# Corner keys of late attention units gathered by GpSimd into one tile, in a vision-transformer layer kernel

## The chip, the cores and the metric

The kernel runs on one core of a Trainium2 chip. The time is the device time of one execution in microseconds (us); several executions are timed and the median counts. TensorE multiplies matrices and transposes (a product with the identity), ScalarE (ACT) and VectorE (DVE) read its results from PSUM, GpSimd (POOL) works on SBUF, SyncE (SP) issues DMAs. The engines run their own instruction streams in order and wait for one another through semaphores.

## The reference

One layer of a vision transformer over 64 images of 197 tokens (196 patches and a class token) with 192 features:

```
h = concat(cls_tok, patches(x) @ W_proj.T + b_proj)
z = layernorm(h)
for e in range(4):                       # 4 experts, 12 heads of 16 features each
    q, k, v = z @ wq[e].T, z @ wk[e].T, z @ wv[e].T
    s = q @ k.T / 4, kept where 0 <= i - j < 64     # sliding window over keys
    outs.append((softmax(s) @ v) @ wo[e].T)
f = concat(outs)
h = h + silu(f @ w_gate.T) * (f @ w_up.T)
z = layernorm(h)
expert = argmax(softmax(z @ gate_w + gate_b - gate_center))
h = h + (gelu(z @ w1[expert] + b1[expert]) @ w2[expert] + b2[expert])
```

## The kernel before

After a prologue (weights are split into a high and a low half-precision part) a loop `Fori` of 32 turns takes two images a turn; an expert stage follows it. A turn projects q, k and v, writes them to SBUF, and SyncE's DMAs (`stack_queries`, `stack_keys`) gather them in the layout that the score products need. Then the attention runs as a pipeline of `UNITS` = 64 units (`unit_of`): 8 groups of 6 heads, and in each group 8 units: first the four of the first 128 queries, then the four "late" ones of the last 69 queries; each has three heads (`HU`) of one image. In what follows a group's units are numbered 0 to 7, the late ones 4 to 7.

In step s of the pipeline each engine does, in this order of its own:

- TensorE: `scores(s)` (the mask and the scores, L706 and L711, into one of three banks), `patch_part` (embedding of the next turn, in early steps only, L263), `turn_p(s - 2)` (transposes of the probabilities, L728 and L731, into one of three banks), `times_v(s - 5)` (products of the turned probabilities with v, at L245 by `product`)
- ScalarE: the copy of the turned probabilities in half precision (`pt_hi`, L838) for unit s - 3, then the exponentials of unit s (`p_ready`, L847)
- VectorE: every fourth step the copy of the output bank to `o_raw` (`o_copied`, L921), then the minimum of the scores of unit s (L928), the low part of unit s - 4 by subtraction (`pt_lo`, L933), and every fourth step the reciprocals (L942)
- GpSimd: for each window of four units `divide(w)`: the sum of two halves of `o_raw` (L874, when `o_copied`), then the multiply with the reciprocals (L880, when `o_rcp_ready`)

The output of four units lies in one PSUM bank, so that the first product of the next window waits for `o_copied`. `scores(s)` waits for the exponentials of unit s - 3, `turn_p(u)` for those of unit u and for `pt_lo` of unit u - 3.

A late query needs keys 65 to 196 (`KWN[1]` = 132). 128 keys fit on the partitions: 69 to 196. The four others (`EDGE`), keys 65 to 68, matter to the first four of the late queries alone. Before, each head of a late unit is therefore transposed twice: once for its first 128 keys, of which four columns are kept (L728), and once for its last 128 (L731); `times_v` then multiplies both with their v, in a high and a low part, four products a head. The v of the edge keys stands in `v[:, img, 1]`, where a DMA at L661 puts it on partitions 0 to 3 and the rest is zero.

Of the kernel before, what the change touches and what calls it, by code (L numbers as in the profile page):

```python
# [52 lines left out]
PTN = (128, TOK - 128 + EDGE)  # L53
PT2 = 2 * (TOK - 128)
# [29 lines left out]
def unit_of(u):  # L84

    return u // 8, u // 4 % 2, u // 2 % 2, u % 2
# [7 lines left out]
def vit_layer(nc, x_t, wp, tok_bias, wqkv, wo, wgu, gate_w, gate_bc, w1, b1, w2, b2, ident, mask_id,  # L94
# [4 lines left out]
    with ExitStack() as ctx:  # L99
# [8 lines left out]
        def sem(name):  # L108
# [61 lines left out]
        pt_late = w1_s[:].rearrange("p s b e n -> p (s b e n)")[:, 0:PR * 2 * HU * PT2].rearrange(  # L170
            "p (r s n) -> p r s n", r=PR, s=2)
        gated = pt_f[:, 0:8 * D].bitcast(F32).rearrange("p (t d) -> p t d", t=4)
# [30 lines left out]
            proj_mm proj_hi proj_lo v_dup stacked0 stacked1 stacked2 scores_mm min_ready p_ready pt_mm pt_hi pt_lo pv_mm  # L203
# [276 lines left out]
        with nc.Block() as block:  # L480
# [20 lines left out]
            def _(dve):  # L501
# [17 lines left out]
                nc.vector.memset(pt_late, 0.0)  # L519

# [59 lines left out]
        def probs(u, hl):  # L580

            if unit_of(u)[1]:
                return pt_late[:, u % PR, hl].rearrange("p (h n) -> p h n", h=HU)
            return pt[:, u % PR, hl, 0:HU * 128].rearrange("p (h n) -> p h n", h=HU)

        def turned_probs(u):
            half = unit_of(u)[1]
            n = PT2 if half else 128
            return bank[T_BANK + u % TR][:, 0:HU * n].rearrange("p (h n) -> p h n", h=HU)[:, :, 0:PTN[half]]

# [4 lines left out]
        LAG_T, LAG_HI, LAG_LO, LAG_PV = 2, 3, 4, 5  # L595
# [32 lines left out]
        with nc.Fori(0, STEPS, hint_back_edge=True) as i:  # L628
            with nc.Block(no_gpsimd_drain=True) as block:

                @block.sync
                def _(sp):
# [25 lines left out]
                    for img in range(PAIR):  # L658

                        sp.wait_ge(S["proj_lo"], v_first + 2 * img + 2)  # L660
                        sp.dma_start(v[0:EDGE, img, 1], v[KW0[1]:KW0[1] + EDGE, img, 0]).then_inc(S["v_dup"], 16)  # L661
# [7 lines left out]
                def _(pe):  # L669
# [46 lines left out]
                    def turn_p(u):  # L716
# [6 lines left out]
                        else:  # L723
                            pe.wait_ge(S["proj_lo"], last_use(T_BANK + u))
                        for j in range(HU):
                            c0, k0 = j * (PT2 if half else 128), j * kn
                            if half:
                                nc.tensor.transpose(turned[:, c0 + rows:c0 + 2 * rows], p_slot(u)[:, k0:k0 + 128],  # L728
                                                    ident_s[0:rows, 0:rows])
                                k0 += EDGE  # L730
                            mm = nc.tensor.transpose(turned[:, c0:c0 + rows], p_slot(u)[:, k0:k0 + 128],  # L731
# [586 lines left out]
```

## Time and profile before

| | us |
|---|---|
| median of 3 runs | 4598.94 (4598.64 to 4599.28) |
| the profiled execution | 4602.34 |
| its span, from the first to the last instruction | 4600.4 |
| TensorE busy | 4002.9 (87%) |
| VectorE busy | 3501.7 (76%) |
| ScalarE busy | 3061.3 (67%) |
| GpSimd busy | 1094.2 (24%) |
| mean granted TensorE clock | 0.968 |

A row of a timeline gives the start in us, the duration, the engine, the line, the operation with what it writes and reads, how many instructions are merged, and in brackets how long the engine sat idle before it and who released it. Durations of products contain the latency of the engine's pipeline; what a product costs the next one is the distance of their starts. PE is TensorE's products, PEld its weight loads.

### The profile page before, as it was taken

How to read it: one execution, taken by the hardware profiler on the slowest of the kernel's cores; microseconds unless marked ns; L12 is line 12 of the kernel's file. 1: busy time of each engine (PE TensorE's matmuls, PEld its weight loads, DVE VectorE, ACT ScalarE, POOL GpSimd, SP SyncE). 2: the span in 40 equal slices, each digit the busy share in tenths (PEclk: the TensorE clock that was granted, in tenths of full speed). 3: DMA queues.
4: the chain of work that ended last, by engine and by line, in shares of the span. 5: the costliest groups of instructions: out<-in, count | busy, mean ns of one | idle time of the engine just before them, and what ended most of it. 6: DMA issues, size and time to landing. Idle time of an engine off the chain costs nothing. (4 is left out here: it accounts for less than half of the span.)

```text
span 4600.4 us, 129415 instructions
## 1 busy us (share of the span) xinstructions
PE 4002.9 (87%) x47470; PEld 3077.7 (67%) x47470; DVE 3501.7 (76%) x8872; ACT 3061.3 (67%) x9620; POOL 1094.2 (24%) x1496
## 2 busy tenths in 40 slices
PE   3889888888888898888888889888888888896998
PEld 2677666666666776666666667666666666774776
DVE  4788777777777887777777778777777777785665
ACT  2777766666777777666666777776666667772433
POOL 0222222222222222222222222222222222221222
PEclk7999999999999999999999999999999999997999
DMA  5122221111111222211111112222111111124664
GB/s 180 38 50 50 50 50 48 45 45 47 45 30 45 50 50 50 50 46 45 46 47 44 31 46 50 50 50 50 45 47 46 46 33 40 48 50 167 223 217 162
DMA packets 241812, 294.02 MB, mean 64 GB/s; under 512 B 56489, under 2 KB 223955, under 8 KB 231554
## 3 DMA queue, kind: packets, MB, share of 16 engines
q1 hardware_dynamic: 217698, 214.47, 18.2%
q10 hardware_dynamic: 4608, 38.73, 2.5%
q0 software_dynamic: 18912, 32.58, 2.0%
q8 instruction: 412, 6.75, 0.6%
q14 instruction: 182, 1.49, 0.1%
HBM read 127.06 MB, written 43.10 MB: 37 GB/s over the span
## 5 line engine op out<-in xcount | busy, mean ns | idle before, releaser
L847 ACT ACTIVATE p_s<-bank,smin 128x128 f32<-128x128 f32 (+1 forms) x6144 | 1825.3, 376 | 228.8 <-DVE smin L928 218.3
L928 DVE TENSOR_REDUCE smin<-bank 128x3 f32<-128x384 f32 (+1 forms) x2048 | 1140.7, 557 | 306.1 <-PE bank L711 271.8
L731 PE MATMUL bank<-ident_s,p_s 128*128 128x128 f32 (+1 forms) x6144 | 1008.6, 252 | 17.7
L731 PEld LDWEIGHTS bank<-ident_s,p_s 128*128 128x128 f32 (+1 forms) x6144 | 727.2, 142 | 89.3 <-issue 60.7
L706 PE MATMUL bank<-masks_s,mask_id_s 128*128 128x384 f16 (+1 forms) x2048 | 676.3, 330 | 30.7 <-DVE qt_f L899 16.3
L711 PE MATMUL bank<-stacks_f 128*128 128x256 f16 (+3 forms) x4096 | 678.8, 247 | 0.0
L728 PE MATMUL bank<-ident_s,p_s 69*128 69x69 f32 x3072 | 508.6, 233 | 140.2 <-DVE pt_f L933 133.4
L874 POOL TENSOR_TENSOR w_s<-o_raw 128x192 f32<-128x192 f32 (+1 forms) x512 | 307.4, 600 | 1242.9 <-DVE o_raw L921 1242.9
L728 PEld LDWEIGHTS bank<-ident_s,p_s 69*128 69x128 f32 x3072 | 399.8, 141 | 260.3 <-issue 235.4
L245 PEld LDWEIGHTS bank<-v_f,w_s 128*69 128x69 f16 x12288 | 549.7, 116 | 25.1 <-issue 3.8
L245 PE MATMUL bank<-v_f,w_s 128*69 128x33 f16 x12288 | 560.8, 186 | 5.8
L933 DVE TENSOR_TENSOR pt_f<-bank,pt_f 128x384 f16<-128x384 f32 x1024 | 557.0, 544 | 0.0
L245 PE MATMUL bank<-zt,wqkv_s 128*128 128x394 f16 x1920 | 404.4, 374 | 174.1 <-PEq L983 164.3
L711 PEld LDWEIGHTS bank<-stacks_f 128*128 128x128 f16 (+1 forms) x4096 | 431.0, 105 | 123.3
L838 ACT CAST pt_f<-bank 128x384 f16<-128x384 f32 x1024 | 505.8, 494 | 0.0
L245 PEld LDWEIGHTS bank<-zt,wqkv_s 128*128 128x128 f16 x1920 | 203.7, 109 | 356.4 <-issue 259.7
L880 POOL TENSOR_TENSOR w_s<-w_s,o_rcp 128x192 f32<-128x192 f32 (+1 forms) x512 | 261.5, 511 | 714.5 <-DVE o_rcp L942 712.0
L933 DVE TENSOR_TENSOR w_s<-bank,w_s 128x219 f16<-128x219 f32 x1024 | 383.5, 377 | 30.0 <-ACT w_s L838 30.0
L838 ACT CAST w_s<-bank 128x219 f16<-128x219 f32 x1024 | 369.3, 361 | 54.6 <-PE bank L731 52.7
L772 PE MATMUL bank<-wgu_s,qt_f 128*128 128x384 f16 (+1 forms) x2304 | 400.6, 326 | 0.0
L921 DVE COPY o_raw<-bank 128x396 f32<-128x396 f32 (+1 forms) x512 | 289.1, 565 | 79.0 <-PE bank L245 53.4
L245 PE MATMUL bank<-v_f,pt_f 128*128 128x33 f16 x6144 | 314.8, 178 | 0.0
(124 smaller groups left out, 5471.2 us busy)
## 6 DMA issues: line engine op xcount, KB each, us to landing
stacks_f<-qt_f SPq DMA_DIRECT2D x768, 73.9 KB, 2.1
stacks_f<-kt_f SPq DMA_DIRECT2D x1536, 36.9 KB, 2.1
wx_t<-wx_d SPq DMA_DIRECT2D x36, 1344.0 KB
x_raw<-x_t_dram ACTq DMA_DIRECT2D x32, 1182.0 KB
rec_t<-rec_d SPq DMA_DIRECT2D x36, 678.0 KB, 4.1
rec_d<-fill_s SPq DMA_DIRECT2D x5, 678.0 KB, 4.1
stacks_f<-w_dram SPq DMA_DIRECT2D x2, 1536.0 KB
wx_d<-w_s SPq DMA_DIRECT2D x8, 384.0 KB
```

Of the source, the lines that this page charges most:

```text
L245: mm = nc.tensor.matmul(psum, stat, mov, start=(n == 0), stop=(n == len(passes) - 1))
L706: nc.tensor.matmul(ps, mask_id_s[:, 0:rows], masks_s[:, m0:m0 + HU * kn], start=True, stop=False)
L711: mm = nc.tensor.matmul(ps[:, j0 * kn:j1 * kn], qst[:, g % QS, two, q0:q0 + rows], kst[:, g % KS, h0 + j0:h0 + j1, k0:k0 + kn], start=Fals ...
L728: nc.tensor.transpose(turned[:, c0 + rows:c0 + 2 * rows], p_slot(u)[:, k0:k0 + 128], ident_s[0:rows, 0:rows])
L731: mm = nc.tensor.transpose(turned[:, c0:c0 + rows], p_slot(u)[:, k0:k0 + 128], ident_s[0:rows, 0:rows])
L772: mm = nc.tensor.matmul(bank[GU_BANKS[tt]][0:rows, 0:2 * D], ot[:, b, zi, c0:c0 + rows], wgu_s[:, s, b, :], start=(b == 0 and s == zi == 0 ...
L838: nc.scalar.copy(probs(u, 0)[:, :, 0:PTN[half]], turned_probs(u)).then_inc(S["pt_hi"], 1)
L847: ins = nc.scalar.activation(p_slot(s)[:, j * kn:j * kn + kn], bank[s % SR][0:rows, j * kn:j * kn + kn], ACT.Exp, scale=-1.0, bias=smin[0: ...
L874: nc.gpsimd.tensor_tensor(mine, o_raw[0:rows, w % 2, :, :, 0:HD], o_raw[0:rows, w % 2, :, :, HD:2 * HD], ALU.add).then_inc(S["o_summed"], 1)
L921: nc.vector.tensor_copy(o_raw[0:rows, w % 2], o_bank(rows)).then_inc(S["o_copied"], 1)
L928: nc.vector.tensor_reduce(least, ps, AX_X, ALU.min).then_inc(S["min_ready"], 1)
L933: nc.vector.tensor_tensor(probs(u, 1)[:, :, 0:PTN[half]], turned_probs(u), probs(u, 0)[:, :, 0:PTN[half]], ALU.subtract).then_inc(S["pt_lo ...
```

## The change

GpSimd copies, for each late unit, the 4 x 4 corners of its three heads (four queries by four edge keys) side by side into `edges`, a tile of which the rest is zero. It does so in step s for unit s - 1, ahead of a division that falls in the same step. TensorE waits for that copy (`edge_ready`), transposes the tile once, which puts head j's edge keys on partitions 4j to 4j + 3, and then each head's last 128 keys. The v of the edge keys is laid out to match: six DMAs in place of two put head j's rows on partitions 4j to 4j + 3. In `times_v` one product with 99 columns (three heads by 33) adds the edge part of all three heads, once for the high and once for the low part. A late unit has four transposes in place of six and eight products in place of twelve; the copy of its turned probabilities has 211 columns in place of 219.

```diff
-PTN = (128, TOK - 128 + EDGE)
-PT2 = 2 * (TOK - 128)
+EDGE_STEP = EDGE
+PTN = (HU * 128, HU * (TOK - 128) + EDGE)
+PT2 = (HU + 1) * (TOK - 128)
...
+        edges = w1_s[:].rearrange("p s b e n -> p (s b e n)")[:, PR * 2 * PT2:PR * 2 * PT2 + XR * 256].bitcast(
+            F32).rearrange("p (r n) -> p r n", r=XR)
...
                 nc.vector.memset(pt_late, 0.0)
+                nc.vector.memset(edges, 0.0)
...
-                        sp.dma_start(v[0:EDGE, img, 1], v[KW0[1]:KW0[1] + EDGE, img, 0]).then_inc(S["v_dup"], 16)
+                        for j in range(HU):
+                            sp.dma_start(v[EDGE_STEP * j:EDGE_STEP * j + EDGE, img, 1, j::HU],
+                                         v[KW0[1]:KW0[1] + EDGE, img, 0, j::HU]).then_inc(S["v_dup"], 16)
...
+                        if half:
+                            pe.wait_ge(S["edge_ready"], edge_of(u) + 1)
+                            nc.tensor.transpose(turned[:, HU * rows:HU * rows + rows], edges[0:rows, u % XR],
+                                                ident_s[0:rows, 0:rows])
                         for j in range(HU):
-                            c0, k0 = j * (PT2 if half else 128), j * kn
-                            if half:
-                                nc.tensor.transpose(turned[:, c0 + rows:c0 + 2 * rows], p_slot(u)[:, k0:k0 + 128],
-                                                    ident_s[0:rows, 0:rows])
-                                k0 += EDGE
-                            mm = nc.tensor.transpose(turned[:, c0:c0 + rows], p_slot(u)[:, k0:k0 + 128],
-                                                     ident_s[0:rows, 0:rows])
+                            k0 = j * kn + kn - 128
+                            mm = nc.tensor.transpose(turned[:, j * rows:j * rows + rows],
+                                                     p_slot(u)[:, k0:k0 + 128], ident_s[0:rows, 0:rows])
...
                         if u == 4:
-                            pe.wait_ge(S["v_dup"], 32)
+                            pe.wait_ge(S["v_dup"], 16 * PAIR * HU)
...
+                        h0 = HG * g + HU * hh
+                        o = o_bank(rows)[:, img, HU * hh:HU * hh + HU, :]
+                        if half:
+                            nc.tensor.matmul(o, probs(u, 0)[:, HU * rows:PT2], v[:, img, 1, h0:h0 + HU, :],
+                                             start=True, stop=False)
                         for j in range(HU):
-                            head = HG * g + HU * hh + j
-                            o = o_bank(rows)[:, img, HU * hh + j, :]
-                            passes = [(probs(u, hl)[:, j, rows * b:rows * b + rows], v[:, img, 2 * half - b, head, :])
-                                      for b in range(1 + half) for hl in range(2)]
-                            mm = product(o, passes)
+                            for hl in range(2):
+                                mm = nc.tensor.matmul(o[:, j], probs(u, hl)[:, j * rows:j * rows + rows],
+                                                      v[:, img, 2 * half, h0 + j, :],
+                                                      start=(hl == 0 and not half), stop=(hl == 1 and not half))
+                        if half:
+                            mm = nc.tensor.matmul(o, probs(u, 1)[:, HU * rows:PT2], v[:, img, 1, h0:h0 + HU, :],
+                                                  start=False, stop=True)
                         mm.then_inc(S["pv_mm"], 1)
...
-                    for w in range(2 * G):
-                        divide(w)
+                    for s in range(PIPE):
+                        u = s - LAG_EDGE
+                        if 0 <= u < UNITS and unit_of(u)[1]:
+                            pool.wait_ge(S["p_ready"], u + 1)
+                            if u >= XR:
+                                pool.wait_ge(S["pt_mm"], u - XR + 1)
+                            nc.gpsimd.tensor_copy(edges[0:EDGE, u % XR, 0:HU * EDGE],
+                                                  split_heads(p_slot(u)[0:EDGE])[:, :, 0:EDGE]
+                                                  ).then_inc(S["edge_ready"], 1)
+                        w = window_at(s, LAG_OC)
+                        if w is not None:
+                            divide(w)
```

`LAG_EDGE` is 1, and `LAG_OC` stays 6. `edge_of(u)` counts the late units. The ScalarE copy and the VectorE subtraction take the same tiles as before, now without a dimension for the head.

## Rows read from the trace of the kernel before

**Rows 1.** Busy time by stretch: one period of eight units.

```profile
core 0: us, PE busy (x) PEld busy (x) DVE busy (x) ACT busy (x) POOL busy (x), PEclk, DMA share, GB/s
2040.23:2049.81 9.58, 8.88 (x139) 7.25 (x135) 8.48 (x21) 9.08 (x33) 2.22 (x4) 1.00 0.22 46
```

**Rows 2.** Timeline of turn 16, scores of unit 1 to scores of unit 4.

```profile
2040.23 0.32 PE L706 MATMUL bank<-masks_s,mask_id_s 128*128 128x384 f16 x1
...
2041.55 0.32 PE L706 MATMUL bank<-masks_s,mask_id_s 128*128 128x384 f16 x1
...
2042.55 0.38 DVE L933 TENSOR_TENSOR w_s<-bank,w_s 128x219 f16<-128x219 f32 x1
2042.66 0.32 PE L706 MATMUL bank<-masks_s,mask_id_s 128*128 128x384 f16 x1
...
2042.84 0.22 DVE L942 RECIPROCAL o_rcp<-o_raw 128x12 f32<-128x12 f32 x1
2043.07 0.52 PE L731 MATMUL bank<-ident_s,p_s 128*128 128x128 f32 x3
2043.19 0.56 DVE L928 TENSOR_REDUCE smin<-bank 128x3 f32<-128x384 f32 x1
...
2043.42 0.56 PE L245 MATMUL bank<-v_f,w_s 128*69 128x33 f16 x12
...
2043.83 0.34 PE L706 MATMUL bank<-masks_s,mask_id_s 128*69 128x396 f16 x1
```

**Rows 3.** Timeline of the same turn, exponentials of unit 5 onward.

```profile
2046.40 0.89 ACT L847 ACTIVATE p_s<-bank,smin 69x132 f32<-69x132 f32 x3 [0.17 <-DVE smin L928]
2046.75 0.56 DVE L928 TENSOR_REDUCE smin<-bank 69x3 f32<-69x396 f32 x1
2046.98 0.25 PE L728 MATMUL bank<-ident_s,p_s 69*128 69x69 f32 x1 [0.28 <-DVE pt_f L933]
...
2047.23 0.55 DVE L933 TENSOR_TENSOR pt_f<-bank,pt_f 128x384 f16<-128x384 f32 x1
...
2047.69 0.21 DVE L942 RECIPROCAL o_rcp<-o_raw 69x12 f32<-69x12 f32 x1
...
2047.92 0.25 PE L728 MATMUL bank<-ident_s,p_s 69*128 69x69 f32 x1
...
2048.05 0.51 POOL L880 TENSOR_TENSOR w_s<-w_s,o_rcp 69x192 f32<-69x192 f32 x1 [1.49 <-DVE o_rcp L942]
...
2048.32 0.31 PE L245 MATMUL bank<-v_f,pt_f 128*128 128x33 f16 x6
2048.48 0.32 PE L706 MATMUL bank<-masks_s,mask_id_s 128*128 128x384 f16 x1
...
2048.64 0.33 PE L711 MATMUL bank<-stacks_f 128*128 128x256 f16 x2
...
2049.81 0.32 PE L706 MATMUL bank<-masks_s,mask_id_s 128*128 128x384 f16 x1
...
2050.00 0.57 DVE L921 COPY o_raw<-bank 128x396 f32<-128x396 f32 x1
...
2050.72 0.56 PE L245 MATMUL bank<-v_f,w_s 128*69 128x33 f16 x12
```

**Rows 4.** GpSimd's timeline in the projection part of the same turn.

```profile
2005.05 4.69 POOL L886 TENSOR_TENSOR x_s<-x_raw,x_s 128x2364 f16<-128x2364 f32 x1 [6.11 <-ACT x_s L826]
2009.67 0.51 POOL L887 COPY h_in<-h_next 128x384 f32<-128x384 f32 x1
2010.12 0.51 POOL L888 COPY h_in<-h_next 69x384 f32<-69x384 f32 x1
```

**Rows 5.** SyncE's timeline (the time to issue), around the duplicates of v.

```profile
2008.38 1.33 SPq L661 DMA_DIRECT2D v_f<-v_f  x2
...
2015.58 3.88 SPq L652 DMA_DIRECT2D stacks_f<-kt_f  x6
2026.71 1.88 SPq L640 DMA_DIRECT2D stacks_f<-qt_f  x3
```

**Rows 6.** Busy time by stretch (columns as in rows 1): projection part of a turn.

```profile
2004.80:2006.60 1.80, 0.02 (x1) 0.00 (x0) 1.15 (x3) 1.80 (x6) 1.55 (x1) 1.00 0.42 85
2008.60:2012.00 3.40, 3.40 (x13) 1.71 (x12) 3.03 (x10) 1.08 (x3) 2.03 (x3) 0.56 0.23 46
```

More of the change, by code:

```diff
@@ L169, in vit_layer @@
         pt = pt_f[:].rearrange("p (r s n) -> p r s n", r=PR, s=2)
-        pt_late = w1_s[:].rearrange("p s b e n -> p (s b e n)")[:, 0:PR * 2 * HU * PT2].rearrange(
+        pt_late = w1_s[:].rearrange("p s b e n -> p (s b e n)")[:, 0:PR * 2 * PT2].rearrange(
             "p (r s n) -> p r s n", r=PR, s=2)
+        edges = w1_s[:].rearrange("p s b e n -> p (s b e n)")[:, PR * 2 * PT2:PR * 2 * PT2 + XR * 256].bitcast(
+            F32).rearrange("p (r n) -> p r n", r=XR)
         gated = pt_f[:, 0:8 * D].bitcast(F32).rearrange("p (t d) -> p t d", t=4)
@@ L202, in vit_layer @@
         names = """patch_mm embedded z1_ready z2_ready z1t_mm z1t_hi z1t_lo z2t_mm z2t_hi z2t_lo var_ready rstd_ready
-            proj_mm proj_hi proj_lo v_dup stacked0 stacked1 stacked2 scores_mm min_ready p_ready pt_mm pt_hi pt_lo pv_mm
+            proj_mm proj_hi proj_lo v_dup stacked0 stacked1 stacked2 scores_mm min_ready p_ready edge_ready pt_mm pt_hi pt_lo pv_mm
             o_copied o_summed o_rcp_ready o_ready ot_mm ot_hi ot_lo gu_mm sig_ready dve_own h_moved
@@ L580, in probs, with edge_of @@
         def probs(u, hl):
-            if unit_of(u)[1]:
-                return pt_late[:, u % PR, hl].rearrange("p (h n) -> p h n", h=HU)
-            return pt[:, u % PR, hl, 0:HU * 128].rearrange("p (h n) -> p h n", h=HU)
+            return pt_late[:, u % PR, hl] if unit_of(u)[1] else pt[:, u % PR, hl, 0:PTN[0]]
         def turned_probs(u):
-            half = unit_of(u)[1]
-            n = PT2 if half else 128
-            return bank[T_BANK + u % TR][:, 0:HU * n].rearrange("p (h n) -> p h n", h=HU)[:, :, 0:PTN[half]]
+            return bank[T_BANK + u % TR][:, 0:PTN[unit_of(u)[1]]]
+        def edge_of(u):
+            return u // 8 * 4 + u % 4
         def split_heads(ap):
             return ap.rearrange("p (h k) -> p h k", h=HU)
-        LAG_T, LAG_HI, LAG_LO, LAG_PV = 2, 3, 4, 5
+        LAG_EDGE, LAG_T, LAG_HI, LAG_LO, LAG_PV = 1, 2, 3, 4, 5
         LAG_OC, LAG_OR = 6, 7
@@ L837, in _ @@
                                 act.wait_ge(S["pv_mm"], u - PR + 1)
-                            nc.scalar.copy(probs(u, 0)[:, :, 0:PTN[half]], turned_probs(u)
+                            nc.scalar.copy(probs(u, 0)[:, 0:PTN[half]], turned_probs(u)
                                            ).then_inc(S["pt_hi"], 1)
@@ L932, in _ @@
                             dve.wait_ge(S["pt_hi"], u + 1)
-                            nc.vector.tensor_tensor(probs(u, 1)[:, :, 0:PTN[half]], turned_probs(u),
-                                                    probs(u, 0)[:, :, 0:PTN[half]], ALU.subtract
+                            nc.vector.tensor_tensor(probs(u, 1)[:, 0:PTN[half]], turned_probs(u),
+                                                    probs(u, 0)[:, 0:PTN[half]], ALU.subtract
                                                     ).then_inc(S["pt_lo"], 1)
```

## The prediction

> **What bounds the kernel now.** The loop over 32 pairs of images takes most of the span, and its attention part is a pipeline of 64 units in which TensorE, VectorE and ScalarE hand each unit round in a fixed order. I read first the busy time of one period of eight units [rows 1]: 9.58 us, of which TensorE is busy 8.88, ScalarE 9.08, VectorE 8.48 and GpSimd 2.22. No engine is full, so a sum of removed busy time would tell little: the period has to be walked. The timeline of that period [rows 2, 3] shows how. Numbering the units of a group of heads 0 to 7 (4 to 7 are the late ones, 69 queries), the rows from 2041.55 to 2043.83 are steps in which TensorE goes from product to scores to transposes without a break: there its work is the limit. The rows at 2046.98 and 2049.81 to 2050.72 are others: TensorE waits for VectorE's subtraction (0.28 us idle before unit 4's transposes), and unit 4's product waits for the copy that empties the output bank. Time saved on TensorE counts in the first kind of step, not in the second. Last I looked at where GpSimd stands in time, because the change makes TensorE wait for it.
>
> **TensorE's saving.** A late unit now has six transposes, whose starts lie 0.0625 us apart (2047.92 to 2048.32 is 0.40 for six) [rows 3]; four remain: -0.125 us. It has twelve value products, 0.41 us from the first to the next scores (2043.42 to 2043.83) [rows 2], 0.0345 each; eight remain, two of them 99 columns wide. No row has 99 columns behind 69-column weights. The mask's product streams 384 columns in 0.16 (2048.48 to 2048.64) [rows 3], so 99 take 0.041. The lower bound is the narrow product's own 0.0345 (the wide one costs nothing more), the upper 0.0345 + 0.041 = 0.075 (one after the other). I take 0.049, near the streaming time, for weights load beside the stream before: 6 x 0.0345 + 2 x 0.049 = 0.305, so -0.11 us. The Trainium skill, "TensorE: Matmul & The Clock Gate", section "LDWEIGHTS (loading the stationary operand)", says that a weight load costs by its columns alone; by it 69-column weights are never dearer than 128-column ones, so that all small products would cost 0.026 and a late unit's saving would be 12 x 0.026 - (6 x 0.026 + 2 x 0.043) = 0.07 and not 0.11; with 20 such savings a turn on the path the sum would come out 25 us higher. The trace disagrees: six products with 128-column weights take 0.16 us, 0.026 each [rows 3], and those with 69 columns take 0.0345.
> Together 0.235 us for each of 32 late units a turn. Walking the period without any new wait, one transposition saving (0.125; the others fall into steps that wait for VectorE) and two product savings (0.22) reach the path: 0.345 a group. In the first 15 steps of a turn, where the patch products ride along, TensorE is the limit throughout and 0.81 us is saved. That gives 0.81 + 6 x 0.345 = 2.9 us a turn, 93 us in all, if GpSimd were free.
>
> **The new wait.** It is not free. GpSimd's queue is now, in step order: copy of unit 4's corners, both halves of the division of the late units before, copy of unit 5, 6, 7, division of units 0 to 3. The copy for unit 5 thus stands behind the division's multiply, which waits for the reciprocal. In the trace unit 5's transposes start at 2047.92 and the multiply only at 2048.05; it ends at 2048.56 [rows 3]. The copy's own input has been ready since 2047.29 (0.89 us of exponentials from 2046.40). Behind TensorE's new wait are queued: unit 5's transposes, the product of unit 2, and the scores of the next group's unit 0, on which VectorE and ScalarE depend.
> The delay: 0.13 (multiply starts after the transposes) + 0.45 (GpSimd's multiply to its next instruction; two of its copies start 0.45 apart though each lasts 0.51 [rows 4]) + the copy + the hand-over. No row of GpSimd is as small as 12 columns on 4 partitions. Its rows of two inputs, 192 columns in 0.51 and 2364 in 4.69 [rows 3, 4], make 1.92 ns a column and 0.14 fixed; the upper bound is the 384-column copy, 0.51; the lower, below that fixed part, 0.10. I take 0.19, near the fixed part since 12 columns add 0.02. The hand-over to TensorE: VectorE's copy of the bank ends at 2050.57 and TensorE starts at 2050.72, 0.15 [rows 3]; for GpSimd I take 0.175, bounds 0.11 and 0.20 (no row has TensorE waiting for GpSimd). So 0.13 + 0.45 + 0.19 + 0.175 = 0.95 us, the first time. [...]
> It happens where a late division precedes: in seven of the eight groups of heads of a turn.
>
> **What a period then takes.** From unit 5's transposes to the next group's, with the longest link each time:
> - four transposes 0.25, product of unit 2 0.15, then scores of unit 0 to VectorE's minimum 0.53 (as 2042.66 to 2043.19) [rows 2], minimum 0.48, late subtraction 0.29 (as 2042.55 to 2042.84), copy of the output bank 0.57 and hand-over 0.15 (2050.00 to 2050.72) [rows 3]: 2.42
> - product of unit 4, 0.305; then two steps of scores, minimum, subtraction, transposes, product: 0.53 + 0.48 + 0.38 + 0.15 + 0.35 (2043.07 to 2043.42) + 0.305 = 2.19: together 2.50
> - scores of unit 4 to minimum 0.55 (0.02 more than above, 12 columns more), minimum 0.48, wide subtraction 0.46, bank copy 0.57, hand-over 0.15, product 0.15: 2.36
> - scores of unit 6 to minimum 0.55, minimum 0.48, subtraction 0.46, reciprocal to multiply 0.36 (2047.69 to 2048.05), multiply 0.45, copy 0.19, hand-over 0.175: 2.67
> Sum 9.95; with the unrounded starts 9.90. Before: 9.58 (2040.23 to 2049.81) [rows 2, 3]. The chain now runs once through every engine, and costs +0.32 a group in spite of the savings in it.
> A turn: -0.81 (opening) + 0.95 (first hold) + 6 x 0.32 (periods between seven holds) - 0.82 (behind the last one: three transposition and four product savings) = +1.24 us; times 32 turns, +40 us.
>
> **The rest.** The other three copies are hidden: unit 5's exponentials end at 2047.29, 0.63 us ahead of its transposes [rows 3], and I take the others for alike; start of GpSimd 0.15 after its releaser (reciprocal's end 2047.90 to 2048.05), copy 0.19 and hand-over 0.175 make 0.51. Should it not fit, each costs its excess only. The copy of unit 4 delays the addition before the multiply by 0.2 us, covered by 1.49 us in which the multiply waits for the reciprocal [rows 3]. ScalarE's copy and VectorE's subtraction lose 8 of 219 columns, under 0.01 us each, beside other work. SyncE issues six duplicating DMAs in place of two, +4 x 0.67 = 2.7 us on its queue [rows 5]; the last key stack behind them ends at 2022.2 and not 2019.46, and that queue next waits until 2026.71, so they are covered; without that cover it would be 2.7 us a turn. The two buffers' memsets come once and add under 1 us.
>
> **Sum.** 4602.3 us (profiled execution) + 40 = 4642; that execution is 3.4 us over the median, so 4639.
>
> **Rivals.**
> A, forecast: the held period, 4639. Its own range: copy 0.10 gives 0.09 less for each of 224 holds, -20 us; copy 0.51 gives +72; wide product 0.0345 or 0.075 gives -0.03 or +0.05 at 20 places a turn, -19 or +33. 4605 to 4700. Chance 0.62.
> B, faster: the hold doesn't form, and all of TensorE's saving stays: 4599 - 93 = 4506. It decides at GpSimd's multiply: were it done before about 2047.5, the copy would be ready when TensorE asks. For it: the multiply waits 1.49 us for a reciprocal that VectorE could give sooner if TensorE's lead moved it; and the hold lets VectorE catch up. Against: 2048.56 in the trace, and VectorE's order puts the reciprocal behind two instructions of the same step. In between (a part of the hold repaid) any time from 4506 to 4590. Chance 0.20.
> C, no change: hold as in A with every open term at its low end (copy 0.10, hand-over 0.11, narrow price for wide products): 224 x 0.155 + 19 = 54 us less than A, 4585; with one of them nearer its middle 4590 to 4608. Chance 0.10.
> D, much slower: TensorE idles some 1.1 us in every period, and the clock falls. After a stretch in which TensorE had almost nothing for 1.8 us the granted clock fell to 0.56, in the projection part of a turn; in the attention part it is 1.00, with idle times of 0.3 [rows 1, 3, 6]. At half clock for one third of each period TensorE-bound steps would add about 0.8 us a group, 200 us for 256 groups: 4840, and with one group in four 4690. The Trainium skill, "TensorE: Matmul & The Clock Gate", section "HAM oscillation — how this bites in real kernels", tells of kernels that lose the clock by waits in every round. Chance 0.08.
>
> **From these the numbers.** Predicted 4639. Range 4585 to 4695: it takes A nearly whole and C, and leaves out most of B and D. A measurement of this kernel can tell 0.2% (9 us) from no change. Faster 0.20 (B), same 0.10 (C), slower 0.70 (A and D).
>
> **What would show it.** In the trace after: TensorE idle about 1.1 us before unit 5's edge transpose, released by GpSimd's copy, in seven groups a turn, and a period of 9.9 us; GpSimd's copy near 0.19 us, its start 0.45 behind the multiply's; eight late products in 0.305. Wrong if the copy takes over 0.3 us, if the clock falls in the attention part, or if the multiply moves ahead so that the hold is under 0.5 us.

## The result: 2.4% slower

The changed kernel takes 4708.94 us, the median of four runs (4702.35 to 4718.34), beside 4598.99 for the kernel before on the same chip: ratio 1.0241, 95% interval 1.0223 to 1.0258. It is slower, as forecast, but by 110 us and not by 40, and outside the range of 4585 to 4695. The profiled execution took 4702.35 us (span 4700.5); its mean granted clock is 0.941, where it was 0.968.

From the page of the changed kernel: busy times, the granted clock by slices, and the groups of the new transpose and of GpSimd's new copy (shapes and count | busy us, mean ns of one | idle us before, and what ended it).

```profile
PE 3907.5 (83%) x41326; PEld 2901.9 (62%) x41326; DVE 3491.1 (74%) x8873; ACT 3051.2 (65%) x9620; POOL 1247.3 (27%) x2520
PEclk7999999999999999999989999999999999997999
L734 PE MATMUL bank<-ident_s,w_s 69*128 69x69 f32 x1024 | 260.1, 254 | 317.9 <-POOL w_s L910 220.1
L910 POOL COPY w_s<-p_s 4x12 f32<-4x12 f32 x1024 | 176.6, 183 | 807.2 <-ACT p_s L861 804.8
```

TensorE is busy for 95 us less than before, at a time that is 100 us longer. What took its place stands in the list of its waits (us in total, times, longest):

```profile
PE bank L734 <- POOL w_s L910: 220.1, 221, 1.2
```

Of 224 holds that were forecast (seven a turn), 221 are seen, 1.0 us each: the first of a turn has 1.2 us of idle time, the six behind it 0.96. One of these, in the timeline of turn 11, is the answer to [rows 3]; the second fence is the same place one period on:

```profile
1451.80 0.21 DVE L966 RECIPROCAL o_rcp<-o_raw 69x12 f32<-69x12 f32 x1
...
1452.15 0.51 POOL L894 TENSOR_TENSOR w_s<-w_s,o_rcp 69x192 f32<-69x192 f32 x1 [1.30 <-DVE o_rcp L966]
...
1452.61 0.31 POOL L910 COPY w_s<-p_s 4x12 f32<-4x12 f32 x2
...
1452.93 0.25 PE L734 MATMUL bank<-ident_s,w_s 69*128 69x69 f32 x1 [0.96 <-POOL w_s L910]
...
1453.37 0.32 PE L713 MATMUL bank<-masks_s,mask_id_s 128*128 128x384 f16 x1
```
```profile
1462.82 0.25 PE L734 MATMUL bank<-ident_s,w_s 69*128 69x69 f32 x1 [0.96 <-POOL w_s L910]
```

GpSimd starts the multiply 0.14 us after the reciprocal's end, the copy of unit 5's corners 0.46 behind the multiply's start, and TensorE starts 0.32 after that (the copy's 0.18 and a hand-over of 0.145). From hold to hold 9.89 us pass.

To see where the 100 us went I split each turn in two: the attention part, from the scores of unit 0 to the last product of unit 63, and the projection part, up to the next turn's scores. The windows below (stretch, length, busy time of each engine with its count, granted clock, DMA share, GB/s) are four attention parts, the first of the kernel before and three of the kernel after; then two projection parts of the kernel after.

```profile
2018.04:2102.04 84.00, 78.39 (x1150) 66.11 (x1151) 70.98 (x171) 73.88 (x260) 21.10 (x34) 1.00 0.22 57
```
```profile
3370.92:3455.66 84.74, 72.62 (x959) 58.36 (x959) 70.62 (x171) 73.40 (x260) 25.91 (x66) 1.00 0.24 60
1412.87:1498.46 85.59, 73.80 (x959) 59.62 (x960) 70.68 (x171) 73.39 (x260) 25.92 (x66) 0.98 0.23 58
2320.62:2409.80 89.18, 77.62 (x958) 62.85 (x959) 70.62 (x171) 73.97 (x260) 25.92 (x66) 0.92 0.23 57
...
1498.46:1542.52 44.06, 34.98 (x226) 20.62 (x224) 28.80 (x85) 16.12 (x32) 9.51 (x9) 0.88 0.10 19
1629.44:1671.83 42.39, 32.90 (x227) 19.90 (x224) 28.66 (x85) 16.13 (x32) 9.52 (x9) 0.96 0.08 16
```

With the full clock (2.4 GHz) all through, an attention part takes 84.74 us, 0.75 more than before. But in 30 of the 32 turns the clock falls to its lower level (1.2 GHz) in some stretches, and the part takes up to 5.3 us more. Summed over the 32 turns:

- the attention parts went from 2688.9 to 2773.1 us, +84. Of that 32 x 0.75 = 24 is the longer walk, the forecast's own mechanism. The other 61 go with the clock: in all, 205 us of the attention parts lie at the lower level, where the kernel before has none.
- the 31 projection parts between turns went from 1323 to 1340 us, +17. They come in two lengths, 44.1 and 42.4 us, and the long one occurs 16 times and not 4 (one of the expectations below has 17 and 5).
- the rest of the span differs by 1 us.

In what follows two of the four sets of runs (e1_mult_later to e4_longer_turn, and e6 to e9_longer_again) were taken in a condition in which the kernel before, too, takes 4693 to 4696 us. The kernel before has no trace in it; in every trace of the other kernels there, each turn has a stall of about 1.3 us between its units 5 and 6, and often a stretch of slow clock right behind it. Ratios are therefore taken within a set, and the slow clock is counted from 20 us into the attention part onward. One of the four executions of e8_filled_again took 16966 us, the others 4769 to 4775, and its ratio is that of the others.

### The profile page after: what moved, and what is told of

Its sections match the earlier page's. It is cut to its first block and busy times, and to the rows that moved or that the text cites. A ratio compares the mean times of both kernels' runs of the same rounds, so it can differ in the third digit from the quotient of the medians.

```text
span 4700.5 us, 119304 instructions
## 1 busy us (share of the span) xinstructions
PE 3907.5 (83%) x41326; PEld 2901.9 (62%) x41326; DVE 3491.1 (74%) x8873; ACT 3051.2 (65%) x9620; POOL 1247.3 (27%) x2520
## 5 line engine op out<-in xcount | busy, mean ns | idle before, releaser
L738 PE MATMUL bank<-ident_s,p_s 128*128 128x128 f32 (+1 forms) x6144 | 908.7, 259 | 31.0 <-DVE pt_f L957 11.8
L713 PE MATMUL bank<-masks_s,mask_id_s 128*128 128x384 f16 (+1 forms) x2048 | 692.8, 338 | 30.8 <-DVE qt_f L923 16.4
L738 PEld LDWEIGHTS bank<-ident_s,p_s 128*128 128x128 f32 (+1 forms) x6144 | 627.2, 147 | 134.1 <-issue 103.6
L718 PE MATMUL bank<-stacks_f 128*128 128x256 f16 (+3 forms) x4096 | 700.4, 253 | 0.0
L734 PE MATMUL bank<-ident_s,w_s 69*128 69x69 f32 x1024 | 260.1, 254 | 317.9 <-POOL w_s L910 220.1
L734 PEld LDWEIGHTS bank<-ident_s,w_s 69*128 69x128 f32 x1024 | 150.2, 147 | 455.3 <-ACT p_s L861 228.4
L852 ACT CAST w_s<-bank 128x211 f16<-128x211 f32 x1024 | 362.2, 354 | 67.4 <-PE bank L738 63.2
L957 DVE TENSOR_TENSOR w_s<-bank,w_s 128x211 f16<-128x211 f32 x1024 | 376.2, 370 | 39.1 <-ACT w_s L852 39.1
L910 POOL COPY w_s<-p_s 4x12 f32<-4x12 f32 x1024 | 176.6, 183 | 807.2 <-ACT p_s L861 804.8
L760 PE MATMUL bank<-v_f,w_s 128*69 128x33 f16 x6144 | 368.7, 188 | 0.0
```

The source lines that it names most:

```text
L713: nc.tensor.matmul(ps, mask_id_s[:, 0:rows], masks_s[:, m0:m0 + HU * kn], start=True, stop=False)
L718: mm = nc.tensor.matmul(ps[:, j0 * kn:j1 * kn], qst[:, g % QS, two, q0:q0 + rows], kst[:, g % KS, h0 + j0:h0 + j1, k0:k0 + kn], start=Fals ...
L734: nc.tensor.transpose(turned[:, HU * rows:HU * rows + rows], edges[0:rows, u % XR], ident_s[0:rows, 0:rows])
L738: mm = nc.tensor.transpose(turned[:, j * rows:j * rows + rows], p_slot(u)[:, k0:k0 + 128], ident_s[0:rows, 0:rows])
L760: mm = nc.tensor.matmul(o[:, j], probs(u, hl)[:, j * rows:j * rows + rows], v[:, img, 2 * half, h0 + j, :], start=(hl == 0 and not half), ...
L852: nc.scalar.copy(probs(u, 0)[:, 0:PTN[half]], turned_probs(u)).then_inc(S["pt_hi"], 1)
```

## The experiments

| kernel | median us | ratio to before in its set | slow clock past 20 us, us in all | undisturbed attention part, us | long projection parts of 31 |
|---|---|---|---|---|---|
| before, b_again, b_third | 4599 to 4602 | | 0, 0, 0 | 83.98 | 4, 3, 4 |
| after | 4708.94 | 1.0241 | 205 | 84.74 | 16 |
| a_again | 4725.74 | 1.0277 [1.0260, 1.0294] | 198 | 84.77 | 27 |
| a_third | 4721.52 (one run) | | 229 | 84.76 | 22 |
| e1_mult_later | 4557.80 | 0.9712 [0.9696, 0.9728] | 0 | 80.8, stall in it | 11 |
| e1_again | 4479.85 | 0.9739 [0.9722, 0.9755] | 0 | 79.62 | 17 |
| e2_filled_hold | 4739.37 | 1.0104 [1.0087, 1.0121] | 0 | 86.2, stall in it | 15 |
| e8_filled_again | 4772.50 | 1.0163 [1.0142, 1.0183] | 0 | 86.3, stall in it | 25 |
| e3_twelve_products | 4624.64 | 0.9862 [0.9839, 0.9884] | 3 | 82.6, stall in it | 15 |
| e4_longer_turn | 4720.18 | 1.0064 [1.0046, 1.0083] | 7 | 84.8, stall in it | 14 |
| e9_longer_again | 4737.09 | 1.0086 [1.0069, 1.0104] | 14 | 85.1, stall in it | 19 |
| e9_third | 4667.32 (one run) | | 0 | 83.97 | 22 |
| e5_hold_alone | 4704.09 | 1.0225 [1.0208, 1.0242] | 0 | 87.30 | 2 |
| e6_long_hold_alone | 4837.63 | 1.0292 [1.0272, 1.0312] | 61 | 89.5, stall in it | 12 |
| e7_hold_twelve | 4910.15 | 1.0465 [1.0439, 1.0491] | 287 | 88.7, stall in it | 17 |
| e7_third | 4790.58 (one run) | | 283 | none; 87.49 with one slow stretch | 13 |

The theory behind the forecast was that the hold costs what the walk of the period says. After the result a second part was needed, that the idle time of the hold lowers the clock. Its rivals were that the lighter load of TensorE lowers it (fewer products), that a longer turn alone does, and, for the projection parts, that the four additional DMAs do.

**Taking the hold away.** The multiply moves one step later in GpSimd's order, behind the corner copy of unit 5; the addition stays. Everything else is the changed kernel.

```diff
-                    def divide(w):
+                    def add(w):
...
+                    def divide(w):
...
                         pool.wait_ge(S["o_summed"], w + 1)
...
                         w = window_at(s, LAG_OC)
                         if w is not None:
+                            add(w)
+                        w = window_at(s, LAG_OR)
+                        if w is not None:
                             divide(w)
```

> The changed kernel with GpSimd's multiply of a division one pipeline step later, so that the corner copy of a group's second late unit runs ahead of it; nothing else differs. Theory (the hold of TensorE behind the multiply costs 0.7 us a turn by itself and pulls the clock down as well): no hold, granted clock 1.00 in the whole attention part, period of eight units about 9.2 us and not 9.9, and the forecast's 2.9 us a turn come out: about 4505 us. Rival 1 (fewer products and transposes thin TensorE's work everywhere and the clock falls for that reason): the clock still falls in the attention part, time 4550 to 4600. Rival 2 (the wait for any GpSimd copy is the trouble, not its place behind the multiply): time stays above 4650.

> The changed kernel with the multiply one step later, once more, beside the changed kernel on one chip. Theory: 2.5 to 3% faster than the kernel before and 4 to 5% faster than the changed one; undisturbed attention part 81.0 us (or 1.3 less on a chip without the early stall, that is 79.7 to 81.1). Rival (its gain of the last call was that chip's): ratio to the kernel before within 0.99 to 1.01.

Measured: 4479.85 us beside 4599.96, and 0.948 of the changed kernel of the same set. The list of waits of e1_again has no wait of TensorE for GpSimd any more, and all 32 attention parts take 79.6 us at the full clock. Waits of e1_again, then one attention part of it:

```profile
POOL w_s L916 <- ACT p_s L861: 955.6, 800, 2.8
PE bank L734 <- DVE pt_f L966: 75.6, 224, 0.6
```
```profile
1345.98:1425.59 79.61, 73.31 (x958) 58.49 (x959) 70.53 (x171) 72.57 (x260) 26.38 (x66) 1.00 0.26 64
```

GpSimd now waits for ScalarE's exponentials, as it should, and unit 4's transposes again wait for VectorE. Fewer products alone do not lower the clock. Ratio and clock came as expected, and both rivals are out. The time of 4505 us that the first of the two texts had did not: it was 4558 in the disturbed set, and 4480 in the undisturbed one, 25 us better than that. The timeline of e1_again has the corner copy and the eight late products:

```profile
1385.28 0.18 POOL L916 COPY w_s<-p_s 4x12 f32<-4x12 f32 x1 [0.82 <-ACT p_s L861]
...
1386.16 0.20 PE L756 MATMUL bank<-v_f,w_s 128*69 128x99 f16 x1
...
1386.20 0.35 PE L760 MATMUL bank<-v_f,w_s 128*69 128x33 f16 x6
...
1386.40 0.21 PE L764 MATMUL bank<-v_f,w_s 128*69 128x99 f16 x1
...
1386.45 0.33 PE L713 MATMUL bank<-masks_s,mask_id_s 128*128 128x384 f16 x1
```

The eight go by in 0.29 us. With six narrow ones at 0.0345 that leaves 0.04 for each wide one, the time its 99 columns stream.

**Filling the hold.** The changed kernel, with six products of 384 columns ahead of the wait in every hold; their result is overwritten. TensorE is kept at work while it would wait, and the hold itself stays.

```diff
+                        if u % 8 == 5 and u > 8:
+                            for _ in range(6):
+                                nc.tensor.matmul(turned[:, 0:384], mask_id_s[:, 0:128], masks_s[:, 0:384],
+                                                 start=True, stop=True)
                         if half:
                             pe.wait_ge(S["edge_ready"], edge_of(u) + 1)
```

> The changed kernel with its hold left as it is, but TensorE runs six products of the mask (384 columns each, 0.16 us, results overwritten) in the hold of each group, ahead of the wait for GpSimd's copy. Theory (the clock falls because TensorE idles 1.2 us in the hold): attention part at granted clock 1.00, its length 84.7 to 85 us a turn, total 4620 to 4640 us. Rival (the clock falls for another reason, or the slower clock is not what costs): clock still below 1.00 in the attention part and 4690 to 4720 us.

> The changed kernel with six products of the mask in each hold, once more on the chip of this call. Theory (idle time in the hold, with the rest, brings the clock down): no slow stretch between 30 and 90 us of a turn, attention part 85.0 us, time 4635 to 4655, 60 to 90 us less than the changed kernel although TensorE does more. Rival: 4700 or more.

The additional work is 6 x 0.16 us, about as long as the idle time. The expected times (4620 to 4640, 4635 to 4655) were missed: 4739 and 4772 us, in sets in which the kernel before takes 4693 and 4696, and the changed kernel did not run in them. The kernel with the filled hold is nearer to the one before than the changed kernel is, 1.010 and 1.016 against 1.024 and 1.028 of other sets, so what the filling saves in time is not shown. The delay is still there: 86.2 us, less the stall of about 1.3, is 84.9, beside 84.74 for the changed kernel. What is firm is the clock: past the first 20 us no slow stretch is left in either of the two traces, against 198 to 229 us in the three of the changed kernel. An attention part of e8_filled_again, its last 62.91 us and then its first 25, which hold the stall, has a clock under 1.00 in the first 25 alone:

```profile
1196.54:1259.45 62.91, 58.46 (x736) 44.55 (x737) 52.98 (x128) 55.41 (x197) 17.98 (x50) 1.00 0.15 32
1171.54:1196.54 25.00, 22.14 (x264) 19.12 (x264) 17.71 (x45) 18.47 (x64) 8.03 (x16) 0.93 0.45 124
```

So the delay of the hold costs the walk, and its idleness costs the clock; the two come apart.

**The products alone.** The kernel of e1 with the narrow products of before, twelve a late unit, on the gathered corners.

```diff
-                        if half:
-                            nc.tensor.matmul(o, probs(u, 0)[:, HU * rows:PT2], v[:, img, 1, h0:h0 + HU, :],
-                                             start=True, stop=False)
...
+                            if half:
+                                for hl in range(2):
+                                    mm = nc.tensor.matmul(o[:, j], probs(u, hl)[:, HU * rows:PT2],
+                                                          v[:, img, 1, h0 + j, :], start=False, stop=(hl == 1))
```

> As the kernel with the later multiply, but with the twelve narrow value products of before in place of eight, so that of TensorE's two savings only the transposes remain. Theory (walk of the period: one transposition saving of 0.125 us a group on the path, none of the products): about 1.1 us a turn less than before, 4563 us, some 58 us more than with eight products. Rival (the transposes are hidden behind VectorE throughout, the products bring it all): 4595 to 4600.

It takes 67 us more than e1_mult_later: 1.8 us in an undisturbed attention part, 60 us over all 32 with their slow stretches, and the rest outside of them. Of what e1 gains over the kernel before in an attention part, 4.37 us (4.0 beside e4_longer_turn, whose attention is that of before, in the same disturbed set), 1.8 thus come from the wide products and 2.2 to 2.6 from the transposes. The expectation had the products about right (58 us) and the transposes at 1.1 us, less than half of that.

**A longer turn alone.** The kernel before, with a VectorE memset of the 1024 columns of `z`, unused at that point, at the end of a turn.

```diff
                         nc.vector.tensor_tensor(h[0:rows, tt, :], h_in[0:rows, tt, :], gu, ALU.add)
+                    nc.vector.memset(z[:], 0.0)
```

> The kernel before with one more memset (1024 columns, about 0.5 to 1.1 us) on VectorE at the end of each turn; attention as before. It asks where 17 us of the projection part come from: in the changed kernel that part of a turn takes 44.1 and not 42.4 us in 17 of 31 turns, before in 5 of 31. Theory (whether the slower clock falls on the projections depends on the length of a turn alone): +16 to +34 us for the memset itself, and the number of long projection parts changes too, up to another 20 us. Rival (those long parts come from the new DMAs or copies): 5 or 6 long parts as before, and the memset's own time alone.

> The kernel before with the memset at the end of a turn, once more: in the call before last it could not be told from that chip's early stall what belonged to it. The kernel before has 3 to 5 of 31 projection parts that are 1.7 us longer, the changed one 16 to 27, and the one with the later multiply 17, though none of them touches the projections. Theory (the length of a turn decides how many are slow): attention part 84.0 us in all turns, more than 8 long projection parts, ratio 1.010 to 1.016. Rival (the new DMAs or copies bring them): 3 to 5 long parts, ratio 1.006 to 1.009.

The first two of these were hard to read because of the stall, seen here in e4_longer_turn at a place where VectorE waits for no semaphore:

```profile
517.50 0.57 DVE L928 TENSOR_REDUCE smin<-bank 69x3 f32<-69x396 f32 x1 [1.64 <-issue]
```

> The kernel before with the memset at the end of a turn, beside the kernel before on one chip. Theory (the length of a turn decides how many projection parts are slow): at least twice as many of the 1.7 us longer ones as the kernel before has on the same chip. Rival: as many as the kernel before, plus or minus two.

By its ratio, 1.0086, e9_longer_again lies with the rival (1.006 to 1.009), by its 19 long parts with the theory, and the two cannot be told apart there. The third, in an undisturbed set with b_third, is clearer, though each is a single run. An attention part and two projection parts of e9_third, then a projection part of b_third:

```profile
1404.95:1488.94 83.99, 78.37 (x1150) 66.09 (x1151) 71.00 (x171) 73.89 (x260) 21.11 (x34) 1.00 0.22 57
...
1488.94:1534.16 45.22, 35.13 (x225) 20.90 (x224) 29.96 (x86) 16.13 (x32) 9.54 (x9) 0.89 0.12 24
1618.15:1661.70 43.55, 33.59 (x225) 20.45 (x224) 29.59 (x86) 16.12 (x32) 9.54 (x9) 0.92 0.11 22
```
```profile
1467.40:1509.86 42.46, 33.62 (x226) 20.44 (x225) 28.67 (x85) 16.11 (x32) 9.53 (x9) 0.92 0.11 22
```

The attention part is untouched, and its clock too: a longer turn doesn't lower it. But the projection part, besides its 1.1 us for the memset, is long in 22 of 31 turns against 4. The kernel takes 65 us more than b_third, of which the memset is 32 x 1.1 = 35 and the long projection parts are 18 x 1.7 = 31. This kernel has no additional DMA, so these aren't needed for the long projection parts.

**A hold alone.** The kernel before, in which TensorE, ahead of unit 5's transposes, waits for the multiply of the division (e5), or for a 12-column GpSimd copy of an otherwise unused tile right behind that multiply (e6). No transposition and no product is saved.

```diff
                             pe.wait_ge(S["proj_lo"], last_use(T_BANK + u))
+                        if u % 8 == 5 and u > 8:
+                            pe.wait_ge(S["o_ready"], u // 8 * 2)
```

In e6 the wait is for `S["edge_ready"]`, which the copy increments.

```diff
                         divide(w)
+                        if w % 2 == 1 and w < 15:
+                            nc.gpsimd.tensor_copy(pad[:, 1], pad[:, 0]).then_inc(S["edge_ready"], 1)
```

> The kernel before with the hold and nothing else: TensorE waits, ahead of the six transposes of a group's second late unit, until GpSimd's multiply of the last division is done; no corner copy, no saving. It measures the wait by itself. Theory (walk of the period with a wait of 0.66 us behind the multiply's start): 3.1 us a turn, 99 us, and the clock falls in the attention part as in the changed kernel, 40 to 80 us more: a ratio of 1.03 to 1.04 to the kernel before. Rival (the hold is mostly repaid in the period, and the clock falls for TensorE's lighter load): ratio 1.00 to 1.02 and clock 1.00 between 30 and 90 us of a turn.

> The kernel before with a hold as long as the changed kernel's: behind the multiply GpSimd copies 12 columns of a tile of its own on 4 partitions, and TensorE waits for that ahead of the six transposes of a group's second late unit. All of TensorE's old work stays. In the hold alone without that copy TensorE idled 0.66 us and the attention part kept its clock; in the changed kernel it idles 0.96 us and the clock falls. Theory A (the length of the hold decides): clock below 1.00 between 30 and 90 us of a turn, 1.035 to 1.05 of the kernel before. Theory B (the hold and TensorE's lighter load are needed together): clock 1.00 there, attention part 88.0 to 88.4 us, ratio 1.028 to 1.033.

Timeline and one attention part of e5_hold_alone:

```profile
1456.97 0.51 POOL L882 TENSOR_TENSOR w_s<-w_s,o_rcp 69x192 f32<-69x192 f32 x1 [1.49 <-DVE o_rcp L944]
...
1457.63 0.25 PE L730 MATMUL bank<-ident_s,p_s 69*128 69x69 f32 x1 [0.66 <-POOL w_s L882]
```
```profile
1416.45:1503.76 87.31, 78.38 (x1150) 66.00 (x1151) 70.95 (x171) 74.45 (x260) 21.07 (x34) 1.00 0.21 54
```

With an idle time of 0.66 us (0.92 once a turn, at the first hold) the clock stays up in all 32 turns, and the kernel pays for the delay alone: 3.33 us an attention part, 104 us in all; the walk had said 3.1 and 99. The 40 to 80 us that the expectation added for the clock did not come. Two attention parts of e6, where the idle time is 0.80 us (1.06 at the first hold):

```profile
1457.14:1546.67 89.53, 78.60 (x1150) 66.00 (x1151) 70.88 (x171) 74.93 (x260) 22.02 (x41) 1.00 0.21 54
1993.13:2087.68 94.55, 83.91 (x1150) 71.00 (x1151) 71.26 (x171) 75.30 (x260) 22.02 (x41) 0.93 0.20 52
```

The clock falls past the first 20 us in 8 of the 32 turns, 61 us in all. Neither theory holds as written: the ratio of 1.0292 is that of B and under A's 1.035, while the clock does fall, which B ruled out, but far less than in the changed kernel. The load of TensorE is the one of before, and so the idle time can suffice without the lighter load. The evidence is thinner than for the filled hold: e6 is of a disturbed set, in which kernels without a hold have 0 to 14 us of such clock (e1, e3, e4, e9), and e5 is of an undisturbed one.

**The hold with twelve products.** The changed kernel with the edit of e3. If the lighter load had a part in the fall of the clock, this one should have less of it.

> The changed kernel with its hold and four transposes, but with twelve narrow value products in a late unit in place of eight: only the load of TensorE differs from the changed kernel, by 0.1 us a late unit. Theory A (the length of the hold decides): the clock falls in the attention part as often as in the changed kernel, some 60 slow stretches, ratio to the kernel before 1.035 to 1.045. Theory B (hold and lighter load together): fewer than half as many, ratio 1.015 to 1.03.

> The changed kernel with twelve products in place of eight and the same hold. In the last call it had 84 slow stretches between 25 and 90 us of a turn, more than the changed kernel (50) on another chip, though TensorE has more to do. Theory (narrow products behind a hold do not keep the clock up): again clearly more than the changed kernel has on the same chip. Rival (the chip made the difference): as many as the changed kernel within 20%.

It has more: 283 us of slow clock beside 229 of a_third in the same set, and 287 in the other set. An attention part of e7_third and one of a_third:

```profile
1316.39:1407.47 91.08, 80.09 (x1086) 66.77 (x1087) 70.73 (x171) 74.09 (x260) 25.94 (x66) 0.93 0.21 55
```
```profile
1684.16:1771.08 86.92, 75.13 (x958) 60.39 (x959) 70.69 (x171) 73.56 (x260) 25.91 (x66) 0.96 0.23 57
```

I had leant to the load here, and that theory fell: TensorE is busier (80.09 against 75.13 us), idles 0.96 us as before, and its clock is lower. The ratio of e7_hold_twelve, 1.0465, lies above even theory A's 1.035 to 1.045. e7_third takes 69 us more than a_third. Some 64 are for the products (attention parts with a single slow stretch take 87.5 and 85.5 us, 2.0 a turn more), (283 - 229) x 0.3 = 16 for the clock, at the 61 us for 205 of the result, and 9 fewer long projection parts give back 15: 65 in sum. These are single traces, so the 54 us of additional slow clock show no more than that the products did not help.

**The controls.** The two kernels again, unchanged, in the two undisturbed sets.

> The kernel before, unchanged, for its trace on the chip of this call. In the four kernels of the call before, the step from unit 5 to unit 6 of a turn took 2.5 to 2.65 us where the two first traces have 1.31. Theory (a stall of that chip, whatever the kernel): on such a chip this kernel shows it too, with time near 4690; on another chip 4599 us and 1.31. Rival (the edits brought it): 1.31 here and in the other traces of this call that leave the opening of the pipeline alone it stays at 2.5.

> The changed kernel, unchanged, on the same chip as the others of this call. Theory: slower than the kernel before by 1.5 to 2.6%, granted clock below 1.00 in the middle of the attention part (30 to 90 us into a turn), where the kernels without the hold, or with the hold filled, never had it. Rival (the clock of the attention part belongs to the chip and not to the hold): no slow stretches between 30 and 90 us here either, or as many in the kernel with the later multiply.

> The kernel before, unchanged. Two calls ran on chips on which it takes 4693 and 4696 us, and there every edited kernel had a stall of 1.3 us ahead of unit 6 of a turn and slow clock 10 to 15 us into the turn. Theory (it is the chip's, not the edits'): where this kernel takes about 4695 us its trace shows 2.5 to 2.65 us from unit 5 to unit 6; where it takes 4600 us, 1.31. Rival: about 4695 us with 1.31.

> The changed kernel, unchanged, beside the one with twelve products on one chip. Theory (as before): 50 to 60 slow stretches of TensorE's clock inside the attention part, beyond those of an early stall if the chip has one.

Neither control of the kernel before met the disturbed condition: both have 1.31 us between units 5 and 6 at 4600 and 4602 us, and that the stall belongs to the condition and not to the edits rests on the edited kernels, which have it in two sets and not in the other two. The kernel before comes within 3 us. The changed one varies by up to 17 us between sets, and it does so in what isn't fixed by its order: the slow clock (198 to 229 us) and the long projection parts (16 to 27); its undisturbed attention part is the same to 0.03 us.

## Why the prediction was right in its direction and wrong in its size

The forecast had the right mechanism for the hold, and its walk of the period holds. The step that failed is the clock: rival D stood beside the sum with a chance of 0.08, and the sum itself has no term for it. It cost 61 of the 100 us. The projection part, with no term either, cost 17, and the end of the turn was mis-sized the other way.

- **The hold forms**, in seven groups a turn. Right: 0.96 us of idle time (1.2 at the first) where 1.1 was written, copy 0.183 (0.19), start behind the multiply's 0.454 (0.45), hand-over 0.145 (0.175, between VectorE's 0.15 and a margin that wasn't needed). Multiply's start to transposes: 0.78, against 0.815.
- **The period** from hold to hold: 9.90 forecast, 9.89 measured, and not by luck: its four links, read from 1452.93 to 1462.82 in turn 11, take 2.43, 2.47, 2.34 and 2.65 us, where the walk has 2.42, 2.50, 2.36 and 2.67.
- **The end of the turn** was the mis-sized term of the walk. Unit 5's transposes of the second group start 0.15 us later in a turn than before (-0.81 + 0.95 = 0.14 forecast), and the six periods add 2.06 (6 x 0.32 = 1.92). From the last hold to the last product, though, 4.08 us pass where the kernel before has 5.54: -1.46, where the forecast had -0.82. The saving was sized about right: e1_again, which has the saving and no hold, takes 4.80 us there, -0.74. What the forecast missed is that the delay of the hold is partly repaid there: e5, which has the hold and no saving, takes 4.77, -0.77. In the kernel before TensorE waits there for VectorE, and unit 62's transposes start 1.34 us behind unit 61's; in e5 that wait is gone and they start 0.56 behind. The wait in the kernel before:

```profile
2097.83 0.25 PE L728 MATMUL bank<-ident_s,p_s 69*128 69x69 f32 x1 [0.62 <-DVE pt_f L933]
```

  In sum +0.75 us a turn and not +1.24, 24 us and not 40.
- **Products and transposes**: eight products in 0.29 us (0.305), the wide one 0.04 (0.049). Right.
- **Without the hold** the forecast had 2.9 us a turn; e1 shows 4.37. Its period is 8.99 us and not 9.23. The step of the walk that failed is the one that let a single transposition saving through. The steps between units 0 and 1 (1.33 to 1.16) and between 6 and 7 (1.35 to 1.18) both shorten by 0.17, the transposition saving among it: there VectorE sat idle for 0.17 us between its reciprocal and the next minimum, and I had counted it as the limit. This row of the kernel before shows it; in e1_again the minimum follows the reciprocal at once (1383.47 and 1383.68):

```profile
2048.08 0.57 DVE L928 TENSOR_REDUCE smin<-bank 69x3 f32<-69x396 f32 x1 [0.17 <-PE bank L711]
```

  This didn't matter to the forecast, since the hold formed, but rival B at 4506 was 26 us too high for what such an order brings (4480).
- **The other copies** are hidden, right: TensorE starts 0.16 us or more after them. SyncE's additional 2.7 us are covered: nothing in the attention part waits for them.
- **Rival D**, the clock, was given a chance of 0.08, as an alternative to A. It is what happened, on top of A. Its price was fair: half clock in one group of four, some 0.8 us each, 51 us; measured 61. What failed is the comparison behind its chance. I set idle times of 1.1 us between two rows, 0.3 at the full clock and 1.8 with a fall [rows 3, 6], and argued as if the case lay with the first. Nothing in the rows said so. (The longest idle time at the full clock was read too low as well: once a turn the kernel before idles 0.62 us, in the row above at 2097.83.) An open question of that kind should have had a chance near one half and the range up to 4700 and beyond. The Trainium skill, "TensorE: Matmul & The Clock Gate", section "HAM oscillation — how this bites in real kernels", tells of a matmul kernel that waits 3 to 5 us for a DMA in each round of its loop and loses the clock each time. The waits here are shorter, and no run has one of the page's length in each round: with 0.96 us the clock falls in the changed kernel and not with the wait filled (e2, e8), with 0.80 it falls a little (e6), and with 0.66 not at all (e5).
- **The projection part** was left out. It had two lengths in the kernel before already (4 long of 31), and this could be read from its windows. A turn of another length changes how often the long one comes: +17 us here, 31 in e9_third. It isn't the length alone: turns of e5 and of the changed kernel both take 129.9 us on average from start to start, and e5 has 2 long ones, the changed kernel 16. Long ones have a lower clock in these kernels (0.88 against 0.92 to 0.96). What decides it is open.

With the terms as measured: 24 + 61 + 17 = 102 us, the 100 by which the profiled executions differ and the rounding. The profiled execution of the changed kernel is the fastest of its four; the medians differ by 110.

**A version that beats both** is e1: 2.6% faster than the kernel before and 5.2% faster than the changed one, measured beside both. It moves one multiply behind one copy in GpSimd's order. The products and transposes saved were worth having; the place of the copy in the queue was what cost.

## What to carry to other kernels

When a small step on an engine with an in-order queue becomes a link between two busy engines, look at what stands ahead of it in that queue: here 0.18 us of copying behind a multiply turned a gain of 120 us into a loss of 110, and swapping the two got it back. A recurring wait can cost twice, once by its delay, which the walk of the timeline gave here to 0.01 us a period (and 0.64 us too high at the end of the turn), and once by the clock. If the rows hold no idle time of the new length, treat the clock as open and let the range say so.

## What the chip showed that I had not expected

- The clock of TensorE fell with a recurring idle time of 0.96 us each 9.9 us (198 to 229 us of slow clock in an execution), less with 0.80 us (61 us, in a disturbed set), and not with 0.66 us. At 0.96 us, more narrow products elsewhere did not help (283 and 287 us); wide ones put into the idle time itself kept it up. The three idle times belong to kernels that differ in other ways too, so no limit follows from them.
- The same program runs 2% longer in some sets, on one and the same chip, with a stall of about 1.3 us at one place of each turn, ahead of which the trace names no semaphore (VectorE idles 1.64 us there, in the row of e4_longer_turn above). Its cause wasn't found.
- A memset that makes each turn 1.1 us longer made the projection part, in which it lies, longer by another 1.7 us in 18 more turns of 31 (e9_third, a single run beside b_third).
